# A two-layer kernel in fp32 split products: the second layer's block loop written out, and the last block's gathers, splits and turns placed otherwise

## The chip, the cores and the metric

One core of a Trainium2 chip. The time is the device time of one execution in microseconds (us); lower is better. Before the change the median of three runs is 2612.52 us (2612.11 to 2613.67).

## The reference

`x` is 32 x 128 x 2048 in fp32. The first layer isn't touched by the change. The second adds to x1 (the first layer's result) the following, x1 and the output being seen as 4096 rows of 2048:

```
z   = grouped conv(x1, 9 taps, 4 groups) + (cond @ c_weight.T) + fside
t   = z[:, perm]                        # columns permuted, then 16 heads of 128
g   = gelu(einsum('bhd,hdm->bhm', t, up))     # up: 16 x 128 x 512
y   = einsum('bhm,hmd->bhd', g, down)         # down: 16 x 512 x 128
out = x1 + y[:, unperm]
```

## The kernel before, in words

Every fp32 product is made of three products in TensorE's fp32r form: a value is split into `hi` (a copy rounded to fp32r) and `lo` (value minus `hi`), and hi x hi, hi x lo and lo x hi are summed in PSUM.

The second layer (`layer1_block`) works on 8 blocks of 512 rows. A block has 16 steps, one per head, so there are 128 steps; the text numbers them by 16k + h. The channel axis of z, with the permutation, is brought to the partitions by way of HBM: z goes transposed to `z_d`, and the rows of a head are gathered from there by an indirect DMA; y is scattered to `y_d` in the same way, loaded again and turned back by transposes.

In step s the engines do the following, each in its own order, written out by hand in five functions `step` (one per engine) that `drive` calls:

- PE (L1445): the conv of unit s + 20 (9 products, `conv`), four transposes of the z before it (`turn_z`), four transposes of the y of unit s - 17, which belongs to the block behind (`turn_y`, L1437), and then for mc = 0 to 3 three down products of step s (`down_part`, into `ps_y`) and three up products of step s + 1 (`up_part`, into `ps_up`). `down_part` for mc 0 waits until ACT has emptied `ps_y` (`y_ready`), `up_part` for mc 0 until DVE has made `t_lo` of its step (`tlo_ready`).
- ACT (L1509): `split_t` (the hi copy of the gathered rows), z out of PSUM with its bias, the hi of x for the conv, then for mc 0 to 2 the gelu of step s + 1, `y_s` (L1546: `ps_y` to SBUF), and the gelu for mc 3. From step 109 on (`late`) it also makes `g_hi` for mc 1 and 3 (L1507).
- DVE (L1623): `split_t` (the lo of the gathered rows, L1580), `take_z`, `take_final` (L1604: the turned y plus x1 into `o_s`), the lo of x, then for mc 0 to 3 `g_hi` (L1615, unless ACT made it) and `g_lo` (L1620).
- POOL (L1357): gathers (L1345) of a step two or three ahead, as `gathered_at` says, and the scatter of y (L1378). The gather of a block's first step waits until all z of the block are in HBM.
- SP (L1301): loads of x1, of y and x1 for the block behind (`load_final`), stores of z and of the result.

The last block differs. With step 107 the last conv is done, with step 108 the last z is turned. Where `early` holds, `split_t` of a step is made a step sooner, between mc 2 and mc 3, on ACT and on DVE. The y of a block can be loaded when all of its 16 steps have been scattered; so at step 112 SP waits for the scatter of step 111, and PE turns the first of these in step 113. After step 127 four loads bring the last block's y, and 16 turns and sums end the kernel.

`drive` writes out step -20 to -1, block 0 and 1, loops twice over two blocks (blocks 2 to 5), and writes out blocks 6 and 7 and two steps behind.

Of the kernel before, what the change touches and what calls it, by code (L numbers as in the profile page):

```python
# [20 lines left out]
H, M = 16, 512  # L21
MC = M // P
RB = 512
BLOCKS = NB * C // RB
SB = RB // C
LEAD = 20


def wait(eng, sem, value):

    if isinstance(value, int) and value <= 0:
        return
    eng.wait_ge(sem, value)


def fp32(ap):
    return ap.bitcast(F32)
# [1013 lines left out]
def layer1_block(nc, block, sh, x1_d, up, down, perm, ident, z_d, y_d, out):  # L1051

    with ExitStack() as ctx:
# [57 lines left out]
        STEPS = BLOCKS * H  # L1111
# [11 lines left out]
        def exists(k, h, offset):  # L1123
            return not isinstance(k, int) or 0 <= H * k + h + offset < STEPS

        def final_exists(k, h, n):
            return not isinstance(k, int) or 0 <= H * (k - 1) + h - n < STEPS - H

        def drive(eng, step):


            for h in range(2 * H - LEAD, H):
                step(-2, h, 0)
            for k in (-1, 0, 1):
                for h in range(H):
                    step(k, h, k % 2)
            with eng.Fori(1, BLOCKS // 2 - 1) as i:
                for parity in range(2):
                    for h in range(H):
                        step(2 * i + parity, h, parity)  # L1140
            for k in (BLOCKS - 2, BLOCKS - 1):
                for h in range(H):
                    step(k, h, k % 2)
            step(BLOCKS, 0, 0)
            step(BLOCKS, 1, 0)
# [56 lines left out]

        def early(k, h):

            return isinstance(k, int) and H * k + h > STEPS - LEAD + 1

        def gathered_at(k, h):


            left = STEPS - (H * k + h) if isinstance(k, int) else STEPS  # L1210
            return {21: (2, 3), 20: (3,), 19: (), 18: (2, 3), 17: (3,)}.get(left, (2,) if left > 21 else (3,))

        def by_scalar(k, h, mc):

# [18 lines left out]
        def before(k, h, n=1):  # L1233

            return (k, h - n) if h >= n else (k - 1, h - n + H)

        def after(k, h):
            return (k, h + 1) if h < H - 1 else (k + 1, 0)
# [148 lines left out]
        @block.tensor  # L1387
        def _(pe):
            def up_part(k, h, mc):
                s = H * k + h  # L1390
                if mc == 0:
                    pe.wait_ge(tlo_ready, s + 1)
                wait(pe, gelu_done, MC * (s - 1) + mc + 1)
                hi, lo = t_pair(k, h)
                for n, (w, t) in enumerate(((w_hi, hi), (w_hi, lo), (w_lo, hi))):
                    mm = nc.tensor.matmul(ps_up[:, mc, :], chunk(w, 2 * h)[:, mc * P:(mc + 1) * P], t,  # L1396
                                          start=(n == 0), stop=(n == 2))
                mm.then_inc(up_done, 1)

            def down_part(k, h, mc):  # L1400
                s = H * k + h
                pe.wait_ge(glo_ready, MC * s + mc + 1)
                if mc == 0:
                    wait(pe, y_ready, s)
                for w, g in ((w_hi, g_hi), (w_hi, g_lo), (w_lo, g_hi)):
                    mm = nc.tensor.matmul(ps_y[:, 0, :], chunk(w, 2 * h + 1)[:, mc * P:(mc + 1) * P], g[:, mc, :],  # L1406
                                          start=(mc == 0 and w is w_hi and g is g_hi),
                                          stop=(mc == MC - 1 and w is w_lo))
                mm.then_inc(down_done, 1)

            def conv(k, h):
                u, j, b, g = conv_unit(k, h)
                if isinstance(k, int) and u < G:
                    pe.wait_ge(sh.cwlo_ready, g + 1)
                pe.wait_ge(xlo_ready, u + 1)
                wait(pe, z_ready, u - 1 if paired(k, h) else u)
                hi, lo = xp_pair[pair_of(k, h)]
                acc = conv_bank(k, h)
                for tau in range(3):
                    for n, (w, x) in enumerate(((cw_hi, hi), (cw_hi, lo), (cw_lo, hi))):  # L1420
                        mm = nc.tensor.matmul(acc, w[:, 3 * g + tau, :], x[:, tau:tau + Q],  # L1421
                                              start=(tau == 0 and n == 0), stop=(tau == 2 and n == 2))
                mm.then_inc(conv_done, 1)

            def turn_z(k, h):
                u, _, _, _ = conv_unit(k, h)
                z = z_pair[pair_of(k, h)]
                if isinstance(k, int) and u == 0:
                    pe.wait_ge(small_in, 32)
                    pe.wait_ge(sh.u_read[1], 4 * QUADS)  # L1430
                pe.wait_ge(z_ready, u + 1)
                wait(pe, zt_ready, u)
                for w in range(4):
                    mm = nc.tensor.transpose(ps_zt[:, 0, w * P:(w + 1) * P], z[:, w * P:(w + 1) * P], id_s[:])  # L1434
                mm.then_inc(zt_done, 1)

            def turn_y(k, h):  # L1437
                v, j, _, _ = final_unit(k, h)
                pe.wait_ge(yt_in[j], 16 * (H // 2 * (k - 1) + h // 2 + 1))
                wait(pe, o_ready, v)  # L1440
                for l in range(4):
                    mm = nc.tensor.transpose(ps_f[:, 0, l * P:(l + 1) * P], yt_s[j][:, l, :], id_s[:])  # L1442
                mm.then_inc(fin_done, 1)

            def step(k, h, parity):  # L1445
                if exists(k, h, LEAD):
                    conv(k, h)
                if exists(k, h, LEAD - 1):
                    turn_z(*before(k, h))
                if final_exists(k, h, 1):  # L1450
                    turn_y(*before(k, h))
                if isinstance(k, int) and H * k + h == -1:
                    pe.wait_ge(wsplit_lo, CHUNKS)
                    pe.wait_ge(z_ready, LEAD)
                for mc in range(MC):
                    if exists(k, h, 0):
                        down_part(k, h, mc)
                    if exists(k, h, 1):
                        up_part(*after(k, h), mc)

            drive(pe, step)
            for v in range(H):
                b, c = v % 4, v // 4
                pe.wait_ge(last_yt_in[c], 16)
                if v == 0:
                    pe.wait_ge(o_ready, STEPS - H)
                    pe.wait_ge(z_ready, STEPS)
                    pe.wait_ge(zt_ready, STEPS)
                    pe.wait_ge(gelu_done, MC * STEPS)
                wait(pe, last_o, v - 3)  # L1470
                for l in range(4):
                    mm = nc.tensor.transpose(last_ps[v % 4][:, l * P:(l + 1) * P], last_yt[c][:, l, b * C:(b + 1) * C], id_s[:])
                mm.then_inc(last_fin, 1)
# [84 lines left out]
        def _(dve):  # L1558
# [14 lines left out]
            def split_t(k, h):  # L1573
                s, j = H * k + h, h % 2
                dve.wait_ge(thi_ready, s + 1)
                wait(dve, up_done, t_users(k, h))
                if isinstance(k, int) and s == STEPS - LEAD + 1:
                    dve.wait_ge(conv_done, STEPS)
                hi, lo = t_pair(k, h)
                nc.vector.tensor_tensor(lo, t_s[j], fp32(hi), ALU.subtract).then_inc(tlo_ready, 1)  # L1580
# [42 lines left out]
            def step(k, h, parity):  # L1623
                if not lead(k) and exists(k, h, 1) and not early(*after(k, h)):
                    split_t(*after(k, h))
                if lead(k):
                    split_x(*after(k, h))
                    for n in chunks_of(k, h):
                        split_weights(n)
                if exists(k, h, LEAD - 1):  # L1630
                    take_z(*before(k, h))
                if final_exists(k, h, 1):
                    take_final(*before(k, h))
                if not lead(k) and exists(k, h, LEAD + 1):
                    split_x(*after(k, h))
                if isinstance(k, int) and H * k + h == -1:
                    split_t(0, 0)
                if exists(k, h, 1):
                    for mc in range(MC):
                        split_g(*after(k, h), mc)  # L1640
                        if mc == MC - 2 and exists(k, h, 2) and early(*after(*after(k, h))):
                            split_t(*after(*after(k, h)))

            drive(dve, step)
            dve.wait_ge(o_ready, STEPS - H)
# [84 lines left out]
```

## Time and profile before

| | |
|---|---|
| median of the runs | 2612.52 us |
| profiled execution | 2614.54 us, span 2612.7 us |
| granted TensorE clock, mean | 0.995 |
| second layer, steps 0 to 127 | from about 1541 to 2582 us of the span |
| a step of blocks 1 to 6 | 8.47 us |
| DMA | 541 MB, 207 GB/s over the span |

The span is what lies between the first and the last instruction of the profiled execution. The page gives each engine's busy time; the chain of waits goes back from the last instruction to what released it; in a timeline a bracket gives the idle time of an engine ahead of an instruction and what ended it. A matmul row's end is modelled (0.39 us each, while they start 0.23 us apart), so for PE the starts are what to read.

### The profile page before, as it was taken

What the parts mean: (1) busy time and instruction counts of PE and PEld (TensorE: products, weight loads), DVE (VectorE), ACT (ScalarE), POOL (GpSimd) and SP (SyncE); (2) the same over time, 40 slices, a digit from 0 to 9 for tenths busy, and PEclk for the clock granted to TensorE, in tenths of its full rate; (3) what the DMA queues carried; (4) which work ended last, traced back from release to release, by engine and by line L of the source; (5) the groups of instructions that cost most, each with busy time, mean ns of one, the idle gap of its engine ahead of it and who ended that gap; (6) DMA issues with size and microseconds to landing.
All of it is one profiled execution on the core that took longest, in us unless ns stands there. A gap on an engine that the chain in (4) does not pass through costs nothing.

```text
span 2612.7 us, 39106 instructions
## 1 busy us (share of the span) xinstructions
PE 2564.3 (98%) x12090; PEld 2106.0 (81%) x12090; DVE 1836.2 (70%) x2667; ACT 1002.5 (38%) x1632; POOL 952.1 (36%) x826
## 2 busy tenths in 40 slices
PE   8999999999999999999999999999999999999997
PEld 6788888888888888887888778888888788888775
DVE  6665555965556754576444768888888888888876
ACT  3221212321122322232222555555555555555573
POOL 2366645466654455232233212222222222222221
PEclk9999999999999999999999999999999999999998
DMA  9955544665545677576455654576767676777687
GB/s 316 317 194 203 197 162 154 235 208 194 192 161 180 222 225 222 160 249 208 150 170 182 204 172 131 158 221 210 224 207 222 206 223 210 223 224 218 210 275 244
DMA packets 417282, 541.03 MB, mean 207 GB/s; under 512 B 36248, under 2 KB 270064, under 8 KB 417072
## 3 DMA queue, kind: packets, MB, share of 16 engines
q1 hardware_dynamic: 314816, 307.40, 39.6%
q10 hardware_dynamic: 78144, 154.27, 15.7%
q0 software_dynamic: 24112, 76.80, 9.3%
q8 instruction: 103, 1.69, 0.3%
q14 instruction: 107, 0.88, 0.1%
HBM read 309.72 MB, written 228.61 MB: 206 GB/s over the span
## 4 chain that ended last, share of the span: by engine, by line
PE 91%; DVE 3%; DMA 3%; issue 2%; SPq 1%; ACT 1%; ACTq 0%; DVEq 0%; POOLq 0%; POOL 0%
PE ps_c L459 45%; PE ps_up L1396 13%; PE ps_y L1406 13%; PE ps_c L1421 9%; PE ps_v L437 4%; PE ps_c L425 2%; PE ps_zt L1434 2%; PE ps_f L1442 2%; DVE w_lo L1002 1%; PE ps_up L1421 1%; DVE ring_lo L949 0%; SPq L85 0%; DMA x_n<-in_up 0%; DMA u_s<-z_d,idx 0%; DMA aggw_d<-agg 0%
## 5 line engine op out<-in xcount | busy, mean ns | idle before, releaser
L459 PE MATMUL ps_c<-w_hi,ring_hi 128*128 128x512 f32 x1792 | 712.8, 398 | 2.1 <-DVE r_early L998 1.2
L459 PE MATMUL ps_c<-w_hi,ring_lo 128*128 128x512 f32 x1792 | 706.9, 394 | 0.0
L459 PE MATMUL ps_c<-w_lo,ring_hi 128*128 128x512 f32 x1792 | 706.7, 394 | 0.0
L609 ACT ACTIVATE ring_hi<-raw_n 128x512 fp32r<-128x512 f32 x382 | 239.6, 631 | 874.3 <-DVE raw_n L940 237.6
L1378 POOL DMA_INDIRECT y_d<-y_s,idx x128 | 145.8, 1139 | 728.5 <-ACT y_s L1546 676.8
L1503 ACT ACTIVATE kern<-ps_up 128x512 f32<-128x512 f32 x512 | 306.7, 599 | 262.1 <-PE ps_up L1396 249.2
L459 PEld LDWEIGHTS ps_c<-w_hi,ring_hi 128*128 128x128 f32 x1792 | 337.8, 188 | 80.5 <-DVE ring_lo L949 3.3
L459 PEld LDWEIGHTS ps_c<-w_hi,ring_lo 128*128 128x128 f32 x1792 | 337.5, 188 | 78.9
L459 PEld LDWEIGHTS ps_c<-w_lo,ring_hi 128*128 128x128 f32 x1792 | 337.8, 189 | 75.6
L1620 DVE TENSOR_TENSOR g_lo<-kern,g_hi 128x512 fp32r<-128x512 f32 x512 | 354.7, 693 | 38.7 <-ACT g_hi L1507 22.2
L998 DVE TENSOR_TENSOR r_early<-ps_c,r_early 128x512 f32<-128x512 f32 x256 | 176.7, 691 | 283.2 <-PE ps_c L459 283.2
L949 DVE TENSOR_TENSOR ring_lo<-raw_n,ring_hi 128x512 fp32r<-128x512 f32 x382 | 342.9, 898 | 18.5 <-ACT ring_hi L609 18.3
L998 DVE TENSOR_TENSOR x_s<-ps_c,x_s 128x512 f32<-128x512 f32 x192 | 132.5, 690 | 204.3 <-PE ps_c L459 204.2
L1615 DVE CAST g_hi<-kern 128x512 fp32r<-128x512 f32 x474 | 203.0, 428 | 84.7 <-ACT kern L1503 78.5
L747 POOL TENSOR_TENSOR s<-raw_n 128x512 f32<-128x512 f32 x64 | 85.3, 1333 | 433.1 <-DMA raw_n<-u_d 318.8
L1406 PE MATMUL ps_y<-g_hi,w_hi 128*128 128x512 f32 x512 | 212.4, 415 | 1.0 <-ACT y_s L1546 1.0
L1406 PE MATMUL ps_y<-g_hi,w_lo 128*128 128x512 f32 x512 | 201.0, 393 | 0.0
L1406 PE MATMUL ps_y<-g_lo,w_hi 128*128 128x512 f32 x512 | 200.0, 391 | 0.0
L1396 PE MATMUL ps_up<-t_hi,w_hi 128*128 128x512 f32 x472 | 187.1, 396 | 5.1 <-DVE t_lo L1580 5.1
L1396 PE MATMUL ps_up<-t_hi,w_lo 128*128 128x512 f32 x472 | 186.1, 394 | 0.0
L1396 PE MATMUL ps_up<-t_lo,w_hi 128*128 128x512 f32 x472 | 184.4, 391 | 0.0
L1345 POOL DMA_INDIRECT u_s<-z_d,idx x128 | 130.3, 1018 | 79.0 <-issue 39.7
(211 smaller groups left out, 3841.2 us busy)
## 6 DMA issues: line engine op xcount, KB each, us to landing
u_d<-raw_n ACTq DMA_DIRECT2D x64, 512.0 KB, 3.3
x_d<-r_early ACTq DMA_DIRECT2D x128, 256.0 KB, 3.5
raw_n<-u_d SPq DMA_DIRECT2D x64, 512.0 KB, 3.6
x_d<-x_s ACTq DMA_DIRECT2D x126, 256.0 KB, 2.7
u_s<-x_d SPq DMA_DIRECT2D x496, 64.0 KB, 2.1
z_d<-x_s SPq DMA_DIRECT2D x120, 256.0 KB, 3.8
rear<-y_d SPq DMA_DIRECT2D x112, 256.0 KB, 3.1
rear<-x_d SPq DMA_DIRECT2D x112, 256.0 KB
```

The costliest lines, as they stand in the source:

```text
L459: mm = nc.tensor.matmul(bank, a[:, dc, :], w[k][:, dc, :], start=(first and dc == 0 and n == 0), stop=(dc == 3 and n == 2), skip_group_che ...
L609: nc.scalar.activation(ring_hi[g % RING][:].rearrange("p a n -> p (a n)"), factor(q, k, p), ACT.Copy).then_inc(hi_ready, 1)
L949: nc.vector.tensor_tensor(ring_lo[g % RING][:].rearrange("p a n -> p (a n)"), factor(q, k, p), fp32(ring_hi[g % RING][:].rearrange("p a n ...
L998: nc.vector.tensor_tensor(r_s[p][blk], bank, r_s[p][blk], ALU.add).then_inc((u_read if on_u else y_read)[p], 1)
L1345: nc.gpsimd.indirect_dma_start(out=t_s[j], out_offset=None, in_=z_d[parity], in_offset=bass.IndirectOffsetOnAxis(ap=idx[:, h:h + 1], axis= ...
L1378: nc.gpsimd.indirect_dma_start(out=y_d[parity], out_offset=bass.IndirectOffsetOnAxis(ap=idx[:, h:h + 1], axis=0), in_=y_s[j][:], in_offset ...
L1396: mm = nc.tensor.matmul(ps_up[:, mc, :], chunk(w, 2 * h)[:, mc * P:(mc + 1) * P], t, start=(n == 0), stop=(n == 2))
L1406: mm = nc.tensor.matmul(ps_y[:, 0, :], chunk(w, 2 * h + 1)[:, mc * P:(mc + 1) * P], g[:, mc, :], start=(mc == 0 and w is w_hi and g is g_h ...
L1421: mm = nc.tensor.matmul(acc, w[:, 3 * g + tau, :], x[:, tau:tau + Q], start=(tau == 0 and n == 0), stop=(tau == 2 and n == 2))
L1503: nc.scalar.activation(g_s[:, mc, :], ps_up[:, mc, :], ACT.Gelu).then_inc(gelu_done, 1)
L1615: nc.vector.tensor_copy(g_hi[:, mc, :], g_s[:, mc, :]).then_inc(ghi_ready, 1)
L1620: nc.vector.tensor_tensor(g_lo[:, mc, :], g_s[:, mc, :], fp32(g_hi[:, mc, :]), ALU.subtract).then_inc(glo_ready, 1)
```

## The change

`drive` writes out all blocks: with whole numbers for k everywhere, no registers, no jump. `early` begins at step 109 instead of 110. `gathered_at` has POOL gather step 112 in step 109 and 113 in step 110 (before: both in step 110). In steps 112 to 128 PE's `turn_y` comes behind the products of mc 1 instead of ahead of all products, and DVE's `take_final` behind `split_g` for mc 1 instead of ahead of that for mc 0.

```diff
--- before.py
+++ after.py
@@ -1131,14 +1131,7 @@
 
             for h in range(2 * H - LEAD, H):
                 step(-2, h, 0)
-            for k in (-1, 0, 1):
-                for h in range(H):
-                    step(k, h, k % 2)
-            with eng.Fori(1, BLOCKS // 2 - 1) as i:
-                for parity in range(2):
-                    for h in range(H):
-                        step(2 * i + parity, h, parity)
-            for k in (BLOCKS - 2, BLOCKS - 1):
+            for k in range(-1, BLOCKS):
                 for h in range(H):
                     step(k, h, k % 2)
             step(BLOCKS, 0, 0)
@@ -1202,13 +1195,16 @@
 
         def early(k, h):
 
-            return isinstance(k, int) and H * k + h > STEPS - LEAD + 1
+            return isinstance(k, int) and H * k + h > STEPS - LEAD
+
+        def turned_later(k):
+
+            return isinstance(k, int) and k >= BLOCKS - 1
 
         def gathered_at(k, h):
 
-
             left = STEPS - (H * k + h) if isinstance(k, int) else STEPS
-            return {21: (2, 3), 20: (3,), 19: (), 18: (2, 3), 17: (3,)}.get(left, (2,) if left > 21 else (3,))
+            return {21: (2, 3)}.get(left, (2,) if left > 21 else (3,))
 
         def by_scalar(k, h, mc):
 
@@ -1447,7 +1443,7 @@
                     conv(k, h)
                 if exists(k, h, LEAD - 1):
                     turn_z(*before(k, h))
-                if final_exists(k, h, 1):
+                if final_exists(k, h, 1) and not turned_later(k):
                     turn_y(*before(k, h))
                 if isinstance(k, int) and H * k + h == -1:
                     pe.wait_ge(wsplit_lo, CHUNKS)
@@ -1457,6 +1453,8 @@
                         down_part(k, h, mc)
                     if exists(k, h, 1):
                         up_part(*after(k, h), mc)
+                    if mc == 1 and final_exists(k, h, 1) and turned_later(k):
+                        turn_y(*before(k, h))
 
             drive(pe, step)
             for v in range(H):
@@ -1629,17 +1627,19 @@
                         split_weights(n)
                 if exists(k, h, LEAD - 1):
                     take_z(*before(k, h))
-                if final_exists(k, h, 1):
+                if final_exists(k, h, 1) and not turned_later(k):
                     take_final(*before(k, h))
                 if not lead(k) and exists(k, h, LEAD + 1):
                     split_x(*after(k, h))
                 if isinstance(k, int) and H * k + h == -1:
                     split_t(0, 0)
-                if exists(k, h, 1):
-                    for mc in range(MC):
+                for mc in range(MC):
+                    if exists(k, h, 1):
                         split_g(*after(k, h), mc)
-                        if mc == MC - 2 and exists(k, h, 2) and early(*after(*after(k, h))):
-                            split_t(*after(*after(k, h)))
+                    if mc == 1 and final_exists(k, h, 1) and turned_later(k):
+                        take_final(*before(k, h))
+                    if mc == MC - 2 and exists(k, h, 2) and early(*after(*after(k, h))):
+                        split_t(*after(*after(k, h)))
 
             drive(dve, step)
             dve.wait_ge(o_ready, STEPS - H)
```

## Rows read from the trace of the kernel before

**Rows 1.** the page: each engine's busy time and share.
```profile
PE 2564.3 (98%) x12090; PEld 2106.0 (81%) x12090; DVE 1836.2 (70%) x2667; ACT 1002.5 (38%) x1632; POOL 952.1 (36%) x826
```
**Rows 2.** chain of waits round step 64: start, duration, what.
```profile
2072.98 2.09 PE ps_c L1421 x9
...
2082.90 3.31 issue
...
2092.26 2.09 PE ps_c L1421 x9
...
2100.73 2.09 PE ps_c L1421 x9
```
**Rows 3.** timeline, PE, step 108: start, duration, what, [idle before, releaser].
```profile
2457.78 0.40 PE L1406 MATMUL ps_y<-g_hi,w_lo 128*128 128x512 f32 x1
2459.09 0.50 PE L1396 MATMUL ps_up<-xp_hi,w_hi 128*128 128x512 f32 x1 [0.92 <-DVE xp_lo L1580]
```
**Rows 4.** timeline, ACT and PE, steps 110 and 111.
```profile
2476.82 0.63 ACT L1497 ACTIVATE t_hi<-u_s 128x512 fp32r<-128x512 f32 x1 [0.93 <-DMA u_s<-z_d,idx]
...
2477.35 0.58 ACT L1546 ACTIVATE y_s<-ps_y 128x512 f32<-128x512 f32 x1
...
2476.48 0.60 PE L1442 MATMUL ps_f<-id_s,rear 128*128 128x128 f32 x4
2478.07 0.47 PE L1406 MATMUL ps_y<-g_hi,w_hi 128*128 128x512 f32 x1 [0.99 <-ACT y_s L1546]
```
**Rows 5.** chain of waits, then timeline of PE, into step 113.
```profile
2488.70 3.02 DMA rear<-y_d
...
2491.77 0.66 PE L1442 MATMUL ps_f<-id_s,rear 128*128 128x128 f32 x4 [1.69 <-DMA rear<-y_d]
2492.18 0.48 PE L1406 MATMUL ps_y<-g_hi,w_hi 128*128 128x512 f32 x1
```
**Rows 6.** timeline, PE, one step of the last block.
```profile
2499.12 0.42 PE L1396 MATMUL ps_up<-xp_hi,w_hi 128*128 128x512 f32 x1
...
2502.41 0.39 PE L1396 MATMUL ps_up<-xp_hi,w_lo 128*128 128x512 f32 x1
...
2504.03 0.60 PE L1442 MATMUL ps_f<-id_s,rear 128*128 128x128 f32 x4
2504.58 0.47 PE L1406 MATMUL ps_y<-g_hi,w_hi 128*128 128x512 f32 x1
...
2505.36 0.41 PE L1396 MATMUL ps_up<-t_hi,w_hi 128*128 128x512 f32 x1
```
**Rows 7.** timeline, ACT, the same step.
```profile
2501.44 0.60 ACT L1503 ACTIVATE kern<-ps_up 128x512 f32<-128x512 f32 x1 [0.79 <-PE ps_up L1396]
2502.07 0.63 ACT L1507 ACTIVATE g_hi<-kern 128x512 fp32r<-128x512 f32 x1
...
2503.85 0.59 ACT L1546 ACTIVATE y_s<-ps_y 128x512 f32<-128x512 f32 x1
```
**Rows 8.** timeline, DVE, the same step.
```profile
2500.10 1.08 DVE L1604 TENSOR_TENSOR results<-ps_f,rear 128x512 f32<-128x512 f32 x1
2501.09 0.42 DVE L1615 CAST g_hi<-kern 128x512 fp32r<-128x512 f32 x1
...
2502.83 0.69 DVE L1620 TENSOR_TENSOR g_lo<-kern,g_hi 128x512 fp32r<-128x512 f32 x1 [0.59 <-ACT g_hi L1507]
2503.46 0.43 DVE L1615 CAST g_hi<-kern 128x512 fp32r<-128x512 f32 x1
...
2504.53 0.69 DVE L1580 TENSOR_TENSOR t_lo<-u_s,t_hi 128x512 fp32r<-128x512 f32 x1
```
**Rows 9.** timeline, PE's first up products of steps 112 and 126, ACT's last y_s.
```profile
2485.00 0.42 PE L1396 MATMUL ps_up<-xp_hi,w_hi 128*128 128x512 f32 x1
...
2574.03 0.41 PE L1396 MATMUL ps_up<-xp_hi,w_hi 128*128 128x512 f32 x1
...
2582.35 0.60 ACT L1546 ACTIVATE y_s<-ps_y 128x512 f32<-128x512 f32 x1 [1.95 <-PE ps_y L1406]
```

## The prediction

> **What bounds the kernel now.** I read the page first: the engines' shares [rows 1] say that PE is nearly always busy, so a time comes from the pace of PE's stream and from the few places where it stops. Then the chain of waits round the loop's back edge [rows 2], then PE's timeline for the last block, where the change sits, looking only for bracketed waits. There are three: step 108 waits for a split [rows 3], step 111 for y_s [rows 4], step 113 for turned-y data [rows 5]. Last, one step of the last block on PE, ACT and DVE side by side [rows 6 to 8]. It shows what no share of busy time shows: that these steps are not bound by PE's work but by two chains that end together.
>
> I number steps by 16k+h. Up to step 107 a step has 33 products and two turns, and PE runs them without a hole (8.47 us from conv to conv [rows 2]); ACT and DVE have slack. From step 108 the conv is gone and from 109 turn_z too. A step is then 24 products at 0.23 us, 5.5 us, and it lasts 6.24 us: U to U' in [rows 6], U being the first up product of a step (2499.12, then 2505.36). The rest is waiting, of two kinds:
> - The y chain. The last product of up mc 2 starts at 2502.41 [rows 6]; gelu, split_t and y_s follow on ACT, y_s starts at 2503.85 for 0.59 [rows 7], and the next step's first down product, which needs ps_y empty, starts at 2504.58 [rows 6]: 2.17 after that up product. PE has six more products for that time (1.61 with the one begun) and then turn_y: transposes start at 2504.03, and the down product only 0.55 later, where behind a turn that came too late to hide anything it needs 0.41 (2491.77 to 2492.18 [rows 5]). So turn_y now lies in a hole that exists anyway.
> - The DVE chain. U, up mc 1, its gelu at 2501.44 and ACT's copy g_hi at 2502.07 [rows 7], g_lo at 2502.83, the cast for mc 2 at 2503.46, its g_lo, split_t at 2504.53 [rows 8], and U' at 2505.36 [rows 6], because up mc 0 waits for tlo_ready. From U to split_t 5.41, from there to U' 0.83. DVE doesn't idle from 2502.83 to the end of this. take_final stands ahead of it (2500.10, followed at 2501.09 by the cast for mc 0 [rows 8]), where g_lo of mc 1 has to wait for ACT's copy anyway: it is free there.
>
> **The change part by part.**
>
> (a) Loop written out. The loop runs i = 1 and 2, so there is one back edge, at step 64. The chain has an "issue" piece of 3.31 on DVE there; PE loses 2.34: 2072.98 to 2092.26 is 19.28 for two steps of 8.47 [rows 2]. Blocks before and behind the loop are already written out and step at the same 8.47, so straight-line code of this density costs PE nothing, and I take the whole −2.34 (bounds: 0, if the stall comes back somewhere, to −2.34). Entry and exit of the loop show no stall to win. The trace's sentence is that one jump stopped DVE for 3.31 us. The Trainium skill speaks to it twice. "Advanced Engine Details and Errata", section Control Flow Timing, gives some 0.05 us to a branch and 0.11 to a compare-and-branch, and by that the edit would be worth about 0.1 us; "Runtime: NRT & Kernel Launch", section Instruction fetch mechanics, says that a taken branch to code outside the small window makes the engine fetch it by DMA first. The trace agrees with the second.
>
> (b) Split of step 109 a step sooner. early() now holds for step 109, so ACT and DVE make it in step 107, behind mc 2. Its gather is issued in step 107 already, as before. PE's stall before up mc 0 of step 108 goes: it starts at 2459.09 where 2457.78 + 0.23 was due [rows 3]: −1.08. What the split now pushes: y_s of step 107, by at most one ACT instruction (some 0.5 from start to start, as in [rows 7] from 2501.44 to 2502.07 and less), under turn_z and turn_y at the head of step 108 (twice some 0.4 of PE), and the g cast for mc 3 by 0.6 on DVE, which down mc 3 needs four products groups later. Cost 0 (bounds 0 to 0.3).
>
> (c) Gather of step 112 in step 109 instead of 110. Before, ACT waits 0.93 for it to land, before split_t, y_s is late, and PE's down product starts 1.59 behind the turn at 2476.48 instead of 0.55 [rows 4]: −1.04. On POOL it is now ahead of the scatter of step 109, behind its wait for all z stores of the block; SP issues these in step 108, as soon as the last turned z is there, and the scatter behind the gather waits for y of step 109 in any case, most of a step later. The gathers of 111, 113 and 114 stay in their steps. Cost 0 (bound: if z were late by a step, the gain is gone, 0).
>
> (d) turn_y and take_final after mc 1, steps 112 to 128. At step 113 the y load of the block behind lands at 2488.70 + 3.02 and PE waits 1.69 for it [rows 5]. It now comes to that turn 2.8 us deeper in the step and in a longer step: −1.7. SP, blocked on the last scatter of the block, and the output store for which take_final waited, come free in time too.
>
> Price on PE: at the step's head nothing is in place of the turn, since the y chain still takes 2.17 from up mc 2. Amid the products the turn takes 0.41 up to the next product's start [rows 5]; I take 0.44, with a little for the products' restart behind transposes. By that up mc 2 and so the y chain are later. By this chain alone a step would be 6.24 + 0.44 = 6.68.
>
> Price on DVE: DVE works in order, and take_final now stands between g_lo of mc 1 and the cast for mc 2, inside the DVE chain. Its start-to-start is 0.99 (2500.10 to 2501.09 [rows 8]); 1.08 is its duration. fin_done is long there (the turn starts 2.1 behind U, take_final 4.3 behind it), and the gelu of mc 2, late by 0.44, still ends before DVE is free. So U to split_t becomes 5.41 + 0.98 = 6.39, and U to U' 6.39 + 0.83 = 7.22. That is longer than 6.68, so the DVE chain decides, and PE will wait some 0.5 before every up mc 0. From U of step 112 to U of step 126 are 14 such intervals (2485.00 to 2574.03 [rows 9]): 14 × 0.98 = +13.7. Bounds: below, the PE price alone, 14 × 0.44 = +6.2; above, both added, 14 × 1.42 = +19.9. I take the middle one because the rows give every link of it. [...]
>
> (e) The tail. Step 127 has only down products; the turn amid them adds 0.44 to the way to the last y_s (2582.35 [rows 9]), and between 126 and 127 the turn no longer lies under y_s: +0.3. Together +0.7 (bounds 0 to 0.9). What follows (last scatter, loads, 16 turns and sums) is untouched.
>
> **Sum.** −2.34 − 1.08 − 1.04 − 1.7 + 13.7 + 0.7 = +8.2. The profiled execution took 2614.54 for a span of 2612.7; with the change 2622.8 (span 2620.9). That execution is 2.0 above the median of the runs, 2612.52, so on the median's footing I say 2620.7.
>
> **The rivals.**
> - Only PE pays (take_final finds room on DVE, for instance because split_t is not what up mc 0 waits for): −6.16 + 14 × 0.44 + 0.7 = +0.7, 2613.2. For it: the two chains end within 0.1 of each other in [rows 6 to 8], so which one decides is a close reading. Against: nothing on DVE can be passed, and the row of U in step 108 [rows 3] shows PE held by just this split. 0.14.
> - Faster: the turn amid the products costs nothing, because the hole at the step's head closes by as much as the turn took; the pace stays 6.24 and only the stalls go: −6.2, 2606.3. It decides if down mc 0 can start right behind up mc 3, that is if y_s is done 0.5 us sooner than now; against it ACT's order, which this change leaves as it is. 0.06.
> - The jump's cost comes back in straight-line code, as fetching spread over the engines: the sum without (a), +10.5, 2623.0. Against: even pace in all written-out blocks. 0.10.
> - The split or gather doesn't help, since another wait stands behind it: +9.2 to +10.3, 2622.3. 0.05.
> - My forecast: 0.65.
>
> **How the numbers follow.** What can be told from no change here is 0.2%, 5.2 us, so slower begins at 2617.7 and faster below 2607.3. Slower: forecast 0.65 (of which 0.02 falls under the bound) + 0.10 + 0.05 = 0.78. Same: 0.14 + 0.02 + 0.01. Faster: 0.05. The range takes in the forecast with 13.7 ± 2.5 (0.18 per step either way) and the two higher cases, and goes down to the PE-only case, of which half lies within: 2613.0 to 2624.5. What is left out holds just under 0.2.
>
> **What would show it.** After: no "issue" piece at step 64 and conv to conv 8.47 through it; no wait at up mc 0 of step 108, nor at down mc 0 of step 111; turn_y of step 113 without a DMA wait; U to U' near 7.2 in steps 112 to 126, with PE waiting for xp_lo or t_lo about 0.5 each time and DVE's take_final right behind g_lo of mc 1. A step of 6.7 there with waits for y_s would prove the first rival; a step of 6.2 the second; a PE wait for "issue" in the written-out blocks the third.

## The result, and the profile after

The changed kernel takes 2623.68 us (median of 8 runs, 2620.89 to 2629.65) beside 2613.82 us for the kernel before (8 runs): ratio 1.0040, 95% interval 1.0031 to 1.0050, so +8.1 to +13.1 us; by the medians it is +9.9 us. The forecast was slower: 2620.7 us, a difference of +8.2 us. The profiled execution after took 2625.44 us. All executions here and below ran at a granted clock of 0.994 to 0.997 but one of the variant "take_final alone", which at 0.654 took 3637.66 us and is left out.

The page after, its span and engines' line:

```profile
span 2623.6 us, 36773 instructions
...
PE 2565.5 (98%) x12090; PEld 2102.1 (80%) x12090; DVE 1838.2 (70%) x2667; ACT 1004.0 (38%) x1632; POOL 961.8 (37%) x826
```

The span is 10.9 us longer, while PE's busy time grew by 1.2 us: the loss is waiting. 2.5 us of it come ahead of everything that the change touches. The first layer is the same code in both kernels, yet the up products of step 0 start as follows, before and after (chain of waits):

```profile
1541.08 5.46 PE ps_up L1396 x12
```

```profile
1543.63 5.46 PE ps_up L1392 x12
```

Two executions differ by so much in the opening (over the nine traces of this document the start lies between 1540.53 and 1543.69); all times below are therefore differences within one trace, or of stretches that start behind the opening.

(a) Round step 64, chain of waits after:

```profile
2075.74 2.09 PE ps_c L1417 x9
...
2092.68 2.09 PE ps_c L1417 x9
```

No "issue" piece, and 8.47 us per step: 2075.74 to 2092.68 is 16.94 for two steps, where [rows 2] have 19.28. The steps keep this pace up to step 107 but for two (8.64 and 8.58, from U of step 81 to U of step 83). In some blocks DVE waits for a store of z to land, 1.0 to 1.5 us in most cases and without a loss for PE; here it waited 2.48 us, ahead of its copy at 2233.16, and was late with t_lo. The variant "take_final alone" has two such places (2.46 and 2.42).

What the "issue" was can be narrowed down by the DMA view. In the 15 us around the back edge (2074 to 2089) the kernel before has

```profile
q8 instruction: 3, 0.05, 1.6%
q14 instruction: 6, 0.05, 0.8%
```

and the changed kernel in the same stretch

```profile
q8 instruction: 1, 0.02, 0.4%
```

(queue and kind, packets, MB, share of the engines' time). So nine packets of instructions arrive round the jump where one does without it. Nor does DVE alone stand there: ACT idles 2.68 us in the kernel before, also "issue", ahead of its t_hi at 2084.85.

(b), (c), (d) PE's timeline at the three places where it waited in [rows 3], [rows 4] and [rows 5] (steps 108, 111, 113):

```profile
2458.47 0.39 PE L1402 MATMUL ps_y<-g_hi,w_lo 128*128 128x512 f32 x1
2458.70 0.40 PE L1392 MATMUL ps_up<-xp_hi,w_hi 128*128 128x512 f32 x1
...
2475.99 0.60 PE L1438 MATMUL ps_f<-id_s,rear 128*128 128x128 f32 x4
2476.55 0.47 PE L1402 MATMUL ps_y<-g_hi,w_hi 128*128 128x512 f32 x1
...
2492.82 0.60 PE L1438 MATMUL ps_f<-id_s,rear 128*128 128x128 f32 x4
```

No bracket is left on these rows. U of step 108 follows its down product after 0.23 instead of 1.31 [rows 3], the down product of step 111 the turn after 0.56 instead of 1.59 [rows 4], and the turn of step 113 starts with its data there.

The price: one step of the last block on PE, ACT and DVE, to be laid beside [rows 6 to 8]:

```profile
2497.84 0.50 PE L1392 MATMUL ps_up<-xp_hi,w_hi 128*128 128x512 f32 x1 [0.31 <-DVE xp_lo L1578]
...
2500.05 0.60 PE L1438 MATMUL ps_f<-id_s,rear 128*128 128x128 f32 x4
...
2503.81 0.47 PE L1402 MATMUL ps_y<-g_hi,w_hi 128*128 128x512 f32 x1 [0.38 <-ACT y_s L1544]
...
2505.05 0.50 PE L1392 MATMUL ps_up<-t_hi,w_hi 128*128 128x512 f32 x1 [0.31 <-DVE t_lo L1578]
```

```profile
2500.24 0.60 ACT L1501 ACTIVATE kern<-ps_up 128x512 f32<-128x512 f32 x1 [0.80 <-issue]
2500.88 0.63 ACT L1505 ACTIVATE g_hi<-kern 128x512 fp32r<-128x512 f32 x1
...
2503.08 0.59 ACT L1544 ACTIVATE y_s<-ps_y 128x512 f32<-128x512 f32 x1
```

```profile
2501.64 0.69 DVE L1618 TENSOR_TENSOR g_lo<-kern,g_hi 128x512 fp32r<-128x512 f32 x1 [1.00 <-ACT g_hi L1505]
2502.25 1.09 DVE L1602 TENSOR_TENSOR results<-ps_f,rear 128x512 f32<-128x512 f32 x1
2503.24 0.43 DVE L1613 CAST g_hi<-kern 128x512 fp32r<-128x512 f32 x1
...
2504.32 0.69 DVE L1578 TENSOR_TENSOR t_lo<-u_s,t_hi 128x512 fp32r<-128x512 f32 x1
```

The reader is to see two things. On DVE take_final (2502.25) now stands between g_lo of mc 1 and the cast for mc 2, and split_t, which has to be done for U', starts 6.48 behind U instead of 5.41. On PE there are two waits where there were none in brackets, 0.38 for y_s and 0.31 for split_t; the second ends last. U to U' is 7.21. Over the 14 intervals and in the tail, after:

```profile
2483.52 0.41 PE L1392 MATMUL ps_up<-xp_hi,w_hi 128*128 128x512 f32 x1
...
2584.62 0.50 PE L1392 MATMUL ps_up<-xp_hi,w_hi 128*128 128x512 f32 x1 [0.30 <-DVE xp_lo L1578]
...
2593.78 0.60 ACT L1544 ACTIVATE y_s<-ps_y 128x512 f32<-128x512 f32 x1 [2.27 <-PE ps_y L1402]
```

2483.52 to 2584.62 is 101.10 against 89.03 in [rows 9], +12.07; from U of step 126 to the last y_s it is 9.16 against 8.32, +0.84.

### The profile page after: what moved, and what is told of

It is laid out like the page before. It is cut to its first block, busy times and chain, and to the rows that moved or that the text cites. A ratio compares the mean times of both kernels' runs of the same rounds, so it can differ in the third digit from the quotient of the medians.

```text
span 2623.6 us, 36773 instructions
## 1 busy us (share of the span) xinstructions
PE 2565.5 (98%) x12090; PEld 2102.1 (80%) x12090; DVE 1838.2 (70%) x2667; ACT 1004.0 (38%) x1632; POOL 961.8 (37%) x826
## 4 chain that ended last, share of the span: by engine, by line
PE 90%; DVE 3%; DMA 3%; issue 2%; ACT 1%; SPq 1%; POOL 0%; DVEq 0%; ACTq 0%; POOLq 0%
PE ps_c L459 46%; PE ps_up L1392 13%; PE ps_y L1402 12%; PE ps_c L1417 9%; PE ps_v L437 4%; PE ps_c L425 2%; PE ps_zt L1430 2%; PE ps_f L1438 2%; DMA raw_n<-in_w_t 1%; DVE results L1602 0%; SPq L85 0%; DVE w_lo L1002 0%; DMA x_n<-in_up 0%; DMA raw_n<-in_lora_b 0%; ACT g_hi L1505 0%
## 5 line engine op out<-in xcount | busy, mean ns | idle before, releaser
L1374 POOL DMA_INDIRECT y_d<-y_s,idx x128 | 152.2, 1189 | 730.6 <-ACT y_s L1544 691.6
```

The costliest lines, as they stand in the source:

```text
L1374: nc.gpsimd.indirect_dma_start(out=y_d[parity], out_offset=bass.IndirectOffsetOnAxis(ap=idx[:, h:h + 1], axis=0), in_=y_s[j][:], in_offset ...
```

## The experiments

All were timed with runs of the kernel before between them, the first four on one chip and the last three on another: its median is 2615.08 us (31 runs) beside the first four and 2614.00 us (21 runs) beside the last three. Each variant has 11 runs, take_final alone 7 and the last one 5.

**The loop alone**, on the kernel before.

```diff
-            with eng.Fori(1, BLOCKS // 2 - 1) as i:
...
+            for k in range(-1, BLOCKS):
```

> The kernel before with the loop over blocks 2 to 5 written out and nothing else. My theory: the only thing to win is the one jump at step 64, so conv to conv is 8.47 us through it and the time falls by 2.34 us (to 2611.5 beside 2613.8). Rival (fetching the longer code costs as much somewhere else): no wait at step 64, but new ones, and a time within 1 us of before. Rival (a branch costs about 0.1 us and the stall was of another kind): the stall near step 64 stays.

2611.88 us, ratio 0.9989 [0.9980, 0.9998], −3.2 us by the medians. The chain of waits at the place:

```profile
2072.26 2.09 PE ps_c L1414 x9
...
2089.21 2.09 PE ps_c L1414 x9
```

The stall is gone, and PE's timeline of the last 25 steps shows no wait that the kernel before doesn't have. The time fits −2.34, but its interval (−5.2 to −0.5) would fit half of it too. That nothing is given back is shown by the trace, not by the time: from U of step 0 to the conv of step 107 it is 895.94 us here and 898.26 in the kernel before, −2.32.

**Split and gather alone**, on the kernel before, its loop kept, turns at the head:

```diff
-            return isinstance(k, int) and H * k + h > STEPS - LEAD + 1
+            return isinstance(k, int) and H * k + h > STEPS - LEAD
...
-            return {21: (2, 3), 20: (3,), 19: (), 18: (2, 3), 17: (3,)}.get(left, (2,) if left > 21 else (3,))
+            return {21: (2, 3)}.get(left, (2,) if left > 21 else (3,))
```

> The kernel before with the loop kept, the split of step 109 a step sooner and the gather of step 112 in step 109; the turns stay at the head of each step. My theory: PE's waits of 0.92 at step 108 and 0.99 at step 111 go, -1.08 and -1.04 between U of step 107 and U of step 112, nothing else changes: -2.1 us. Rival (another wait stands behind one of them): -1 us or 0, and a wait of another kind in its place.

2612.97 us, ratio 0.9991 [0.9983, 1.0000], −2.1 us. On PE's timeline U of 108 and of 111 carry no wait, and the one of step 113 is what is left:

```profile
2458.73 0.40 PE L1396 MATMUL ps_up<-xp_hi,w_hi 128*128 128x512 f32 x1
...
2490.05 0.66 PE L1442 MATMUL ps_f<-id_s,rear 128*128 128x128 f32 x4 [1.42 <-DMA rear<-y_d]
```

From the conv of step 107 to U of step 112 it is 34.85 us here and 37.03 in the kernel before: −2.18, expected −2.12.

**take_final last**, the experiment on which of the two prices decides. PE is left as changed, and only DVE's step of the changed kernel is edited:

```diff
-                    if mc == 1 and final_exists(k, h, 1) and turned_later(k):
+                    if mc == MC - 1 and final_exists(k, h, 1) and turned_later(k):
```

> The changed kernel, but DVE's take_final behind the g split of mc 3 and so behind split_t, outside DVE's chain; PE's turn stays amid the products. My theory (two prices, DVE's decides): U to U' falls from 7.22 to 6.68, the PE price alone, with PE waiting for y_s only; 14 intervals, about 7.5 us less than the changed kernel, +0.8 us against before (2614.6 beside 2613.8). Rival (the turn amid PE's products is what costs, wherever take_final stands): U to U' stays near 7.2 and the time near that of the changed kernel, +10.

2618.84 us, ratio 1.0014 [1.0005, 1.0023], +3.8 us: 6.1 us less than the changed kernel's +9.9, though not down to +0.8. PE's timeline of one step, and the last wait of it:

```profile
2503.20 0.42 PE L1392 MATMUL ps_up<-t_hi,w_hi 128*128 128x512 f32 x1
...
2505.05 0.40 PE L1392 MATMUL ps_up<-t_hi,w_lo 128*128 128x512 f32 x1
2505.40 0.63 PE L1438 MATMUL ps_f<-id_s,rear 128*128 128x128 f32 x4
...
2509.21 0.47 PE L1402 MATMUL ps_y<-g_hi,w_hi 128*128 128x512 f32 x1 [0.41 <-ACT y_s L1544]
...
2509.99 0.41 PE L1392 MATMUL ps_up<-xp_hi,w_hi 128*128 128x512 f32 x1
...
2586.51 0.63 PE L1438 MATMUL ps_f<-id_s,rear 128*128 128x128 f32 x4 [1.50 <-DVE results L1602]
```

U to U' is 6.79 here and 6.77 on the mean of 13. The wait for split_t is gone, the one for y_s stays (0.41): PE's price alone. The miss against 6.68 has a place too: the turn should follow the product of 2505.05 by 0.23, and starts at 2505.40, 0.12 late. It waits for the take_final before it, which now comes in the next step:

```profile
2504.17 1.08 DVE L1602 TENSOR_TENSOR results<-ps_f,rear 128x512 f32<-128x512 f32 x1
```

And at the end, with no up products between, the same wait is 1.50. Both belong to this variant, not to the turn's place, and they make up the miss of 3.0 us: 14 times 0.09, and 1.7 at the end, where from U of step 126 to the last y_s it is 10.86 here and 9.16 in the changed kernel.

**take_final alone.** In the changed kernel PE's turn is back at the head of every step:

```diff
-                if final_exists(k, h, 1) and not turned_later(k):
+                if final_exists(k, h, 1):
                     turn_y(*before(k, h))
...
-                    if mc == 1 and final_exists(k, h, 1) and turned_later(k):
-                        turn_y(*before(k, h))
```

> The changed kernel, but PE's turn_y back at the head of every step; only DVE's take_final is behind mc 1. My theory: DVE's chain alone sets U to U' at 7.2 as in the changed kernel, with the whole wait (some 0.9) at up mc 0 and none for y_s; the wait of step 113 for the turned-y data is back in part. U of 112 to U of 126 about 101.7, +8.2 us against before. Rival (PE's move is the cause, take_final's place is free): U to U' 6.2, and -4.4 us against before.

2622.51 us, ratio 1.0032 [1.0021, 1.0043], +7.4 us (expected +8.2). PE's timeline:

```profile
2502.34 0.63 PE L1438 MATMUL ps_f<-id_s,rear 128*128 128x128 f32 x4 [0.48 <-DVE results L1600]
...
2503.91 0.50 PE L1392 MATMUL ps_up<-t_hi,w_hi 128*128 128x512 f32 x1 [0.24 <-DVE t_lo L1576]
...
2511.07 0.50 PE L1392 MATMUL ps_up<-xp_hi,w_hi 128*128 128x512 f32 x1 [0.24 <-DVE xp_lo L1576]
```

U to U' is 7.16 and 7.19 in turn, 101.53 from U of 112 to U of 126 (expected 101.7). So DVE's order alone makes the long step, with not one product of PE displaced. The wait is seen at the turn (for the take_final before it) as well as at U, which I had put at U only. And step 113's turn waits 1.72 for its data again, the whole wait and not a part of it as I had expected.

**Both behind mc 0**, in the changed kernel.

```diff
-                    if mc == 1 and final_exists(k, h, 1) and turned_later(k):
+                    if mc == 0 and final_exists(k, h, 1) and turned_later(k):
```

(on PE and on DVE)

> The changed kernel with turn_y and take_final both behind mc 0 instead of mc 1. My theory: on DVE take_final now falls into the wait for ACT's copy g_hi of mc 1 (0.6 idle, and 0.4 more because the cast for mc 0 starts earlier), so DVE's chain is back at 5.4 and only PE's price is left: U to U' 6.77, as with take_final last, about 6.3 us less than the changed kernel in the 14 intervals; without the 1.5 us wait at the end that take_final last brought, some 2 us above before. Rival (take_final costs DVE's chain its 0.98 wherever it is ahead of split_t): U to U' 7.2.

2614.94 us, ratio 1.0001 [0.9992, 1.0010], +0.9 us (expected some +2): nine of the ten us are gone by moving two instruction groups by one mc. DVE's timeline, then PE's:

```profile
2504.95 0.69 DVE L1618 TENSOR_TENSOR g_lo<-kern,g_hi 128x512 fp32r<-128x512 f32 x1
2505.56 1.08 DVE L1602 TENSOR_TENSOR results<-ps_f,rear 128x512 f32<-128x512 f32 x1
2507.08 0.69 DVE L1618 TENSOR_TENSOR g_lo<-kern,g_hi 128x512 fp32r<-128x512 f32 x1 [0.45 <-ACT g_hi L1505]
```

```profile
2502.94 0.42 PE L1392 MATMUL ps_up<-t_hi,w_hi 128*128 128x512 f32 x1
...
2509.59 0.41 PE L1392 MATMUL ps_up<-xp_hi,w_hi 128*128 128x512 f32 x1
```

take_final starts at 2505.56, and DVE still idles 0.45 before g_lo of mc 1: it lies in the wait for ACT's copy, as the theory had it. U to U' is 6.65 here (expected 6.77), and 6.65 − 6.21 = 0.44 is PE's price as the prediction had it.

**Only the turn of step 113 moved**, and that behind mc 0; the rest as in the changed kernel.

```diff
-            return isinstance(k, int) and k >= BLOCKS - 1
+            return isinstance(k, int) and H * k + h == STEPS - H + 1
...
-                    if mc == 1 and final_exists(k, h, 1) and turned_later(k):
+                    if mc == 0 and final_exists(k, h, 1) and turned_later(k, h):
```

> The changed kernel, but only the one turn that has to wait for its data (step 113) is moved, behind mc 0 with its take_final; all others stay at the head. My theory: all four gains (2.34, 1.08, 1.04 and 1.7) and one PE price of 0.44 to 0.53: U of 112 to U of 126 about 87.7 instead of 89.0, -5.8 us against before, faster than both kernels. Rival (the late turn only shifts the wait to the next turn or to take_final, whose store lands as late as before): -4.4 us, with a wait of over 1 us in step 113 or 114.

2609.02 us, ratio 0.9984 [0.9975, 0.9993], −5.0 us (expected −5.8, within the interval of −6.5 to −1.8): faster than both kernels. PE's U of steps 112, 113, 114 and 126:

```profile
2480.52 0.42 PE L1392 MATMUL ps_up<-xp_hi,w_hi 128*128 128x512 f32 x1
...
2486.76 0.42 PE L1392 MATMUL ps_up<-t_hi,w_hi 128*128 128x512 f32 x1
...
2493.42 0.42 PE L1392 MATMUL ps_up<-xp_hi,w_hi 128*128 128x512 f32 x1
...
2567.93 0.42 PE L1392 MATMUL ps_up<-xp_hi,w_hi 128*128 128x512 f32 x1
```

6.24, then 6.66 for the one step with the turn amid, and 87.41 in all instead of 89.03. No wait of over 0.39 is left in steps 108 to 127.

**And split_t behind mc 1 in the last block**, on ACT and on DVE, beside the one moved turn:

```diff
                 for mc in range(MC - 1):
                     if exists(k, h, 1):
                         gelu(*after(k, h), mc)
-                if exists(k, h, 2) and early(*after(*after(k, h))):
-                    split_t(*after(*after(k, h)))
+                    if mc == 1 and exists(k, h, 2) and early(*after(*after(k, h))):
+                        split_t(*after(*after(k, h)))
...
-                    if mc == MC - 2 and exists(k, h, 2) and early(*after(*after(k, h))):
+                    if mc == 1 and exists(k, h, 2) and early(*after(*after(k, h))):
```

> As the kernel with the one moved turn, and in the last block split_t on ACT and DVE stands behind mc 1 instead of mc 2. My theory of the y chain (gelu mc 2, split, y_s in ACT's order set it): y_s starts 0.13 sooner behind U, U to U' falls from 6.2 to 6.1 and DVE's chain ends 1 us before it is needed: 17 steps, -2.2 us more, -8.0 against before. Rival (down products, not ACT's order, set the start of y_s, or the gelu of mc 2, later by 0.4, holds up DVE): U to U' 6.2 or more, no gain.

2603.69 us, ratio 0.9962 [0.9948, 0.9975], −10.3 us (expected −8.0, within the interval of −13.6 to −6.5; the median is of five runs only). Beside the kernel with the one moved turn the traces show −4.0 from the conv of step 107 to the last y_s (expected −2.2), the medians −5.3. ACT's timeline, then PE's:

```profile
2506.07 0.61 ACT L1495 ACTIVATE t_hi<-u_s 128x512 fp32r<-128x512 f32 x1
2506.59 0.58 ACT L1501 ACTIVATE kern<-ps_up 128x512 f32<-128x512 f32 x1
2507.07 0.59 ACT L1544 ACTIVATE y_s<-ps_y 128x512 f32<-128x512 f32 x1
```

```profile
2502.62 0.40 PE L1392 MATMUL ps_up<-xp_hi,w_hi 128*128 128x512 f32 x1
...
2507.50 0.60 PE L1438 MATMUL ps_f<-id_s,rear 128*128 128x128 f32 x4
2507.85 0.48 PE L1402 MATMUL ps_y<-g_hi,w_hi 128*128 128x512 f32 x1
...
2508.63 0.40 PE L1392 MATMUL ps_up<-t_hi,w_hi 128*128 128x512 f32 x1
```

split_t (2506.07) now lies ahead of gelu mc 2, and y_s starts 4.45 behind U where it was 4.73 [rows 6, 7]; the turn at the step's head is followed by its down product after 0.35, so that nothing is waited for. U to U' is 5.98 on the mean (6.01 and 5.95 in turn) instead of 6.21. I had expected 6.1 from a y_s sooner by 0.13; it came sooner by 0.28, because gelu mc 2 starts 3.97 behind U and y_s 0.48 later. With that no wait is left on PE in these steps, and its own stream is the bound.

## Why the prediction was right

- **(a) the jump**, −2.34: 16.94 against 19.28, −2.34, and −3.2 (ratio's interval −5.2 to −0.5) by itself on the chip. So the 0.1 that is estimated from the figures in the Trainium skill's "Advanced Engine Details and Errata", Control Flow Timing, is not what this jump costs. That the stall is code being fetched is not shown, since the trace says "issue", but the instruction packets speak for it: 9 and 8 of them in 2074 to 2089 in the two traces with the loop, 1 or 2 in the seven without. The prediction names DVE alone; ACT stood for 2.68 at the same place.
- **(b) the split**, −1.08: U of step 108 comes 10.04 behind the conv of step 107 (2448.66) instead of 11.12 (2447.97), −1.08. What it pushed cost nothing.
- **(c) the gather**, −1.04: U of 110 to U of 111 is 6.23 instead of 7.26, −1.03.
- **(d) the turn's wait and its price**, −1.7 + 13.7 = +12.0: measured +12.07 from U of step 112 to U of 126. That DVE's chain decides and PE's doesn't was the reading that the sign hung on, and the two chains ended within 0.1 of each other. The pair of experiments settles it: with DVE's move alone the step is 7.18, with PE's alone (take_final out of the chain) 6.65 to 6.77, with both 7.21. The prices don't add; the longer chain sets the step.
- Two links of the DVE chain were off and cancelled. U to split_t grew to 6.48, not 6.39, because PE, starting from a standstill at U, has its gelu of mc 1 2.40 behind U instead of 2.32; and from split_t to U' it is 0.73, not 0.83, since in the kernel before U' was held by PE's stream and not by split_t: the prediction's "because up mc 0 waits for tlo_ready" is wrong for that kernel, where no bracket stands before U' [rows 6]. That 7.22 was met by 7.21 is in this part luck. PE's wait at U is 0.31 and the rest of it, 0.38, stands at the down product, both of which I had said would come as "some 0.5" at U.
- **(e) the tail**, +0.7: +0.84.
- **Sum**: −2.34 − 1.08 − 1.03 + 12.07 + 0.84 = +8.46 by these terms, and what follows the last y_s took 29.9 instead of 30.4 us. The rest of the span's 10.9 is 2.55 ahead of step 0 and +0.48 that I had not foreseen between it and step 107: 0.20 in the first step, 0.28 in the two steps with DVE's wait for a store. The measured median lies 3.0 us above the 2620.7 forecast: 1.3 because the kernel before measured 2613.82 in eight runs and 2612.52 in the three that I had; the other 1.7 lie within the interval of the ratio. 2623.68 is 0.8 below the range's upper end, and nearer to the rivals at 2622.3 and 2623.0 than to my 2620.7, so the time alone would not have told them apart; the traces do.
- The rivals: "only PE pays" had a time of +0.7 and is what the variant behind mc 0 measures, +0.9. "Faster" would have needed y_s 0.5 sooner; the last experiment got 0.28 by ACT's order and saved 0.23 a step. "The jump's cost comes back" is in no trace: from U of step 0 to the conv of step 107 the traces of five of the seven kernels without the loop agree within 0.03 us (895.93 to 895.96), and the 0.26 and 0.55 more of the other two stand where DVE waits for a store of z. "Another wait behind split or gather" falls with the second experiment.

## What to carry to other kernels

A wait that happens once in a block is to be cured in the step where it happens: with the same other gains, and the turn behind mc 0, the kernel is 5.0 us faster when it is moved in one step and 0.9 slower when it is moved in all (9.9 slower behind mc 1 in all). Before moving an instruction, lay one step of all engines side by side and look for what stands directly behind its new place: take_final was free where DVE waited for ACT's copy and cost its full start-to-start of 0.98 per step one place further on, though DVE was no busier. And where two chains end together, shortening one should show little, which no experiment here tried by itself; the gain of 0.23 us a step came only when ACT's order let y_s be made sooner and DVE's split was moved with it.

## What was not expected

- The interval from U of step 121 to U of 122 is longer by 0.3 in four of nine traces: 7.53 after (7.20 its neighbours), 6.48 before (6.2), and so with split and gather alone and with take_final alone; in the other five it isn't. In the kernel before the chain of waits shows 0.41 of "issue" on DVE there, ahead of g_lo of mc 1. What it is stays open.
- Identical code in the opening puts step 0 of the second layer up to 3.2 us apart in nine traces, more than the smallest effects here. Single terms of this size could be read from the traces, behind the opening, and not from single times.
